# First stage of a graph network kernel: GpSimd takes over small table work from VectorE, the fall test moves, and fewer count columns

## The reference, cut to what matters

```python
h = jnp.maximum(_layernorm(x, axis=-1), 0.0)
x = x + _L0_gnn_ref(h, src, dst, ...)     # hn = layer_norm(h); ft = hn @ W_att; softmax over each
                                          # destination's edges of <ft[src], ft[dst]>; sum of ft[src]; MLP
h = jnp.maximum(_layernorm(x, axis=-1), 0.0)
x = x + _L1_gnn_ref(h, src, dst, ...)     # four convolutions over the same edges
```

## Time and profile before

| | us |
|---|---|
| median of 3 executions | 3775.62 |
| lowest and highest of them | 3770.89, 3781.33 |
| the profiled execution | 3790.5 |
| its span, first to last instruction | 3788.6 |
| of it, first stage with its barrier | 117.67 |

### The profile page before, as it was taken

One profiled execution on the slowest core, in us unless ns is written; L12 is line 12 of the kernel. 1 busy time (PEld: TensorE's weight loads), 2 busy tenths in 40 slices (PEclk: granted clock), 3 DMA queues, 4 the chain that ended last, 5 costly groups with the idle time before them and its releaser, 6 DMA issues. The chain is left out here.

```text
span 3788.6 us, 59184 instructions
## 1 busy us (share of the span) xinstructions
PE 3354.5 (89%) x20346; PEld 2097.6 (55%) x20346; DVE 2355.1 (62%) x3512; ACT 1776.8 (47%) x4853; POOL 2445.6 (65%) x2604
## 2 busy tenths in 40 slices
PE   5788888888888888888888787999999999999999
PEld 4566666666666666666655554444544454445444
DVE  8788888888888888888865574222422242224223
ACT  4788888888888878787744353000200020002000
POOL 2577777777777777777777001777277737764775
PEclk7688888888888888888887798999999999999999
DMA  7443334333333333334332415888688868877886
GB/s 207 125 108 103 107 104 107 104 107 104 107 104 107 104 107 104 107 104 124 103 85 60 62 51 169 254 254 256 215 255 254 253 215 254 256 248 229 259 264 192
DMA packets 491674, 599.98 MB, mean 158 GB/s; under 512 B 61546, under 2 KB 422613, under 8 KB 491103
## 3 DMA queue, kind: packets, MB, share of 16 engines
q1 hardware_dynamic: 355798, 337.71, 29.3%
q0 software_dynamic: 82960, 172.57, 18.4%
q10 hardware_dynamic: 52632, 86.13, 6.3%
HBM read 488.79 MB, written 109.00 MB: 158 GB/s over the span
## 5 line engine op out<-in xcount | busy, mean ns | idle before, releaser
L1001 POOL DMA_INDIRECT fts<-ft_tab,src_all x1568 | 1481.2, 945 | 477.7 <-issue 477.1
L2702 PE MATMUL cv_acc<-cv_cnt,cv_parts 128*128 128x512 bf16 x3960 | 864.0, 379 | 0.0
L2453 POOL DMA_INDIRECT cv_slots<-hs_tab,slot_idx x640 | 604.8, 945 | 195.1 <-issue 195.1
L1033 DVE TENSOR_TENSOR ohk<-iota_ps,key_cols 128x784 bf16<-128x784 f32 x704 | 651.1, 966 | 5.5
L2702 PEld LDWEIGHTS cv_acc<-cv_cnt,cv_parts 128*128 128x128 bf16 x3960 | 387.2, 98 | 464.6
L1457 PE MATMUL agg_ps<-terms,oh 128*64 128x141 f32 x2744 | 557.1, 378 | 75.6 <-DVE terms L1070 75.3
L1457 PEld LDWEIGHTS agg_ps<-terms,oh 128*64 128x64 f32 x2744 | 483.2, 189 | 116.3 <-DVE terms L1070 105.4
L1218 ACT ACTIVATE dist_l<-lo_iota,low 128x128 bf16<-128x128 f16 x1760 | 533.1, 387 | 16.5 <-ACT low L1213 0.4
L1397 PE MATMUL adj_ps<-ohk,ohl 128*128 128x196 bf16 x2816 | 378.2, 261 | 89.5 <-ACT strip L1270 46.8
L1270 ACT CAST strip<-adj_ps 128x392 bf16<-128x392 f32 x704 | 334.0, 474 | 239.5 <-PE adj_ps L1400 200.4
L2702 PE MATMUL cv_acc<-raw,cv_parts 128*128 128x512 bf16 x1920 | 420.9, 379 | 0.0
(11 more groups left out here) (350 smaller groups left out, 3592.1 us busy)
## 6 DMA issues: line engine op xcount, KB each, us to landing
cv_cnt<-adj SPq DMA_DIRECT2D x44, 2176.0 KB
cv_cnt<-adj SPq DMA_DIRECT2D x44, 2048.0 KB
raw<-adj SPq DMA_DIRECT2D x44, 2048.0 KB
adj<-strip ACTq DMA_DIRECT2D x176, 392.0 KB
fts<-ft_tab,src_all POOLq DMA_INDIRECT x1568
win<-ft_tab SPq DMA_DIRECT2D x196, 65.0 KB
hs_tab<-cv_hs ACTq DMA_DIRECT2D x24, 448.0 KB, 3.5
cv_slots<-hs_tab,slot_idx POOLq DMA_INDIRECT x640
```

Of the source, the lines that this page charges most:

```text
L1001: nc.gpsimd.indirect_dma_start(fts[u][:, k, :], None, ft_tab[:, :], bass.IndirectOffsetOnAxis(src_all[:, n, k:k + 1], 0)).then_inc(gathere ...
L1033: nc.vector.tensor_tensor(ohk[:, k.s, at, :], key_no.unsqueeze(1).to_broadcast([P, QC, KEYS]), columns(key_cols, k)[:, at].unsqueeze(2).to ...
L2453: nc.gpsimd.indirect_dma_start(slots[n % RING][:, e, :], None, hs_tab[:, :], bass.IndirectOffsetOnAxis(rows_at, 0)).then_inc(slots_in[n % ...
L2702: last = nc.tensor.matmul(a[:, 0:width], parts[:, r, b, :], cnt[q][:, 0:width // SUB, (b - b0) * SUB:(b - b0 + 1) * SUB], start=(b == 0 an ...
```

## The change

GpSimd makes what VectorE made in `spot_columns`, `rows`, `schedule` and most of `oddities`. It does the first ahead of its two conversions, and the others right after them and ahead of the fetches. Where VectorE had one fused instruction of two operations with a scalar per partition, GpSimd has separate ones: `rows` subtracts the centre with a tensor_tensor over all 2048 columns first. On VectorE `find_falls` moves from cycle 5 to after the loop, followed by one reduction over the odd marks (`count_odd`), both ahead of the last `turned_features`; the rest of `oddities` (`finish`) stays behind it. Counts, bounds and odd marks run over NHD = 1408 strips in place of NH = 1568.

```diff
-CQ = ((0, 393), (393, 392), (785, 392), (1177, 392))
+CQ = ((0, 353), (353, 352), (705, 352), (1057, 352))
...
-        thr = sb("thr", [P, NH + 1], FP16, c)
+        thr = sb("thr", [P, NHD + 1], FP16, c)
...
+            def spot_columns():
+                link(nc.gpsimd.tensor_scalar(side[:, 1:2], place[:], float(WD), None, ALU.is_ge))
...
+                last.then_inc(s["spots_made"], 1)
+
+            def rows():
+                pool.wait_ge(s["dst_f"], 1)
+                link(nc.gpsimd.tensor_scalar(centre[:], dst_f[:, :, 0], float(MID), None, ALU.add))
+                link(nc.gpsimd.tensor_tensor(dst_f[:], dst_f[:], centre[:].unsqueeze(2).to_broadcast([GH, 2, GE]), ALU.subtract))
+                for half in range(2):
+                    for a in range(2):
+                        last = nc.gpsimd.tensor_scalar(
+                            group_rows[:, half, 2 * a, :].rearrange("g (c p) -> g c p", p=P),
+                            dst_f[:, half, :].rearrange("g (p c) -> g c p", p=P)[:, a * (GC // 2):(a + 1) * (GC // 2), :],
+                            float(MID), None, ALU.min)
+                link(last)
+                for a in range(2):
+                    last = nc.gpsimd.tensor_tensor(group_rows[:, :, 2 * a + 1, :], group_rows[:, :, 2 * a, :],
+                                                   group_rows[:, :, 2 * a, :], ALU.mult)
+                last.then_inc(s["rows_made"], 1)
+
+            def schedule():
+                pool.wait_ge(s["ends_in"], 7 * 16)
+                nc.gpsimd.memset(delta_f[:], 0.0)
...
+            def oddities():
+                spans, strips = odd[:, 0:NG], odd[:, NG:NG + NHD]
+                pool.wait_ge(s["starts_made"], 1)
+                nc.gpsimd.tensor_tensor(strips, start_f[:, 1:NHD + 1], start_f[:, 0:NHD], ALU.subtract)
...
+                link(nc.gpsimd.tensor_tensor(spans, last_f[:], base_f[:], ALU.subtract))
+                nc.gpsimd.tensor_scalar(spans, spans, float(WD - 1), None, ALU.is_gt)
+                nc.gpsimd.tensor_scalar(strips, strips, float(SW - COARSE) / COARSE, None, ALU.is_gt
+                                        ).then_inc(s["odd_made"], 1)
+            spot_columns()
             pool.wait_ge(s["by_src_in"], 96)
             nc.gpsimd.tensor_copy(src_f[:], by_src[:]).then_inc(s["src_f"], 1)
             pool.wait_ge(s["by_dst_in"], 96)
             nc.gpsimd.tensor_copy(dst_f[:], by_dst[:]).then_inc(s["dst_f"], 1)
+            rows()
+            schedule()
+            oddities()
...
             def find_falls():
+                dve.wait_ge(s["ends_in"], 7 * 16)
...
-            def oddities():
...
+            def count_odd():
+                dve.wait_ge(s["odd_made"], 1)
                 link(nc.vector.tensor_reduce(irr_part[:], odd[:], AX.X, ALU.add))
+
+            def finish():
                 dve.wait_ge(s["base_summed"], 1)
...
-                if i == 1:
-                    dve.wait_ge(s["pool_const"], 2)
-                    spot_columns()
                 if i == 3:
-                    schedule()
-                if i == 4:
-                    rows()
-                if i == 5:
-                    find_falls()
+                    turned_spots()
+            find_falls()
+            count_odd()
             turned_features(NB - 1)
-            oddities()
+            finish()
```

More of the change, by code:

```diff
@@ L342, in _ @@
             nc.gpsimd.tensor_copy(ident_bf[:], ident[:]).then_inc(s["pool_const"], 1)
+            def spot_columns():
+                link(nc.gpsimd.tensor_scalar(side[:, 1:2], place[:], float(WD), None, ALU.is_ge))
+                link(nc.gpsimd.tensor_scalar(side[:, 0:1], side[:, 1:2], -float(WD), None, ALU.mult))
+                link(nc.gpsimd.tensor_tensor(place[:], place[:], side[:, 0:1], ALU.add))
+                link(nc.gpsimd.tensor_scalar(place[:], place[:], -float(MID), None, ALU.add))
+                link(nc.gpsimd.tensor_scalar(side[:, 0:1], side[:, 1:2], -1.0, 1.0, ALU.mult, ALU.add))
+                link(nc.gpsimd.tensor_tensor(spot_cols[:, 4:5], place[:], place[:], ALU.mult))
+                nc.gpsimd.tensor_scalar(spot_cols[:, 4:5], spot_cols[:, 4:5], -1.0, 1.0, ALU.mult, ALU.add)
+                for a in range(2):
+                    link(nc.gpsimd.tensor_tensor(spot_cols[:, 2 * a:2 * a + 1], side[:, a:a + 1], place[:], ALU.mult))
+                    nc.gpsimd.tensor_scalar(spot_cols[:, 2 * a:2 * a + 1], spot_cols[:, 2 * a:2 * a + 1], 2.0, None, ALU.mult)
+                    last = nc.gpsimd.tensor_scalar(spot_cols[:, 2 * a + 1:2 * a + 2], side[:, a:a + 1], -1.0, None, ALU.mult)
+                last.then_inc(s["spots_made"], 1)
@@ L511, in turned_sources @@
                                           ).then_inc(s["turned_out"], 1)
[L513 to L524, removed]
@@ L526, in schedule, with turned_spots, find_falls @@
-            def schedule():
+            def turned_spots():
                 dve.wait_ge(s["spots_turned"], 1)
                 nc.vector.tensor_copy(spots[:], base_ps[0:5, 0:P])
+            def find_falls():
                 dve.wait_ge(s["ends_in"], 7 * 16)
[L530 to L539, removed]
@@ L541, in rows @@
-            def rows():
-                dve.wait_ge(s["dst_f"], 1)
-                link(nc.vector.tensor_scalar(centre[:], dst_f[:, :, 0], float(MID), None, ALU.add))
-                for half in range(2):
-                    for a in range(2):
-                        last = nc.vector.tensor_scalar(
-                            group_rows[:, half, 2 * a, :].rearrange("g (c p) -> g c p", p=P),
-                            dst_f[:, half, :].rearrange("g (p c) -> g c p", p=P)[:, a * (GC // 2):(a + 1) * (GC // 2), :],
-                            centre[:, half:half + 1], float(MID), ALU.subtract, ALU.min)
-                link(last)
-                for a in range(2):
-                    last = nc.vector.tensor_tensor(group_rows[:, :, 2 * a + 1, :], group_rows[:, :, 2 * a, :],
-                                                   group_rows[:, :, 2 * a, :], ALU.mult)
-                last.then_inc(s["rows_made"], 1)
```

30 lines of the change are left out of this document (17 added, 13 removed).

## The result

| | before | after |
|---|---|---|
| median, us (7 executions each, taken in turn) | 3777.27 | 3787.55 |
| ratio after to before, 95% interval | | 1.0036 (1.002 to 1.0052) |
| profiled execution's span | 3788.6 | 3797.8 |
| first stage, start of the span to the first instruction of the next stage | 117.67 | 127.92 |
| attention, from there to some 2080 us | 1961.33 | 1961.08 |

A forecast was written before the change was run, and what follows sets the result against it. The first stage was taken to be bound by a full VectorE, which GpSimd's new work would hold: counts +9.8, oddities +4.4, pipeline −2.5, end 0, sum +11.7 us on the median 3775.6, so 3787.3 us; range 3774 to 3797.

The forecast's parts named there:

- Stage for stage, 1 us for 1 us: An earlier or later end of the first stage moves the whole rest of the kernel by the same amount.
- The stage's end: Last gap of VectorE: 5.4 us of work fits into 5.52, term 0; up to 1.5 us lost if TensorE is fast.
- The pipeline: From some 58 us ScalarE's three waits for VectorE go, a gain of 2.5 us.
- The reason given for moving the fall test: Left in cycle 5 of the pipeline, find_falls' 3.6 us would have been the next thing waited for.
- Fewer columns: One tenth fewer columns saves 1.9 us over 28 count steps, plus 0.2 for `thr` and starts.
- The counts: GpSimd's `rows` and `schedule`, 11.5 us, hold VectorE's count steps; 1.7 absorbed, so counts end 9.8 us later.
- The factor 1.85 for two operands: GpSimd's two-operand price, taken from VectorE's ratio of 1.771 to 0.957 us: 1.75 us per 1000 columns.
- TensorE follows: At the counts' end TensorE may finish 2 us behind VectorE, covered by the statistics, so no added cost.
- rival D: Dearer two-operand price, and TensorE, starved in the counts, falls to lower speed: +15 to +22 us, chance 0.21.
- Oddities: GpSimd's `oddities`, 4.6 us, holds VectorE's coefficients and edge keys: +4.4 us after 0.2 for shorter starts and `thr`.
- its last way to be wrong: GpSimd's instructions wait in VectorE's place, which would cost only the fetches' slack.
- C: The forecast case itself, GpSimd's work holding VectorE: +9 to +15 us, 3785 to 3791 us, chance 0.38.

The follow-up runs named there:

- e3: The changed kernel with only `rows` moved behind GpSimd's last fetch; ratio to the kernel before 1.0009, first stage from first count step 103.28 us (changed kernel 114.18).
- e8: The changed kernel with the four minima of `rows` reading 512 neighbouring columns in place of every eighth; first stage from first count step 113.77 us (changed kernel 114.18).
- e6: As e5, but with the fall test back in cycle 5 of the pipeline; first stage from first count step 103.24 us, 0.3 above e5.
- e2: The kernel before with only the counts, bounds and odd marks cut to 1408 strips; ratio to before 1.0003, first stage from first count step 101.17 us (before 103.57).
- e4: The changed kernel with strip bounds in PSUM as float32, each count step three plain-rate VectorE instructions; these took 693 ns beside `rows`, 692 with GpSimd idle.
- e1: The changed kernel with `rows`, `schedule` and `oddities` behind GpSimd's last fetch; ratio to the kernel before 1.0002, first stage from first count step 107.24 us.
- e9: As e5, with the fall test too behind the last turned features; ratio to the kernel before 1.0004, first stage from first count step 99.76 us.
- e10: The changed kernel with the fall test and reduction behind the last turned features, GpSimd's part untouched; first stage from first count step 113.14 us (changed kernel 114.18).
- e5: As e1, with the reduction over odd marks behind the last turned features; ratio to the kernel before 1.0003, first stage from first count step 102.97 us.
- e7: The kernel before with four GpSimd memsets of 98 x 2048 float32 added beside the counts; first statistics 29.38 us after the first count step, 9.0 later than before.

## Why the prediction was right, point by point

**Stage for stage, 1 us for 1 us:** held, 1961.33 and 1961.08 us for the attention.

**The stage's end:** held. SP waits 3.7 us for its last store again. The gap was filled to the edge: VectorE's features started at 118.50 us, TensorE's transposes had ended at 117.13 + 1.27 = 118.40. Of this trace the term of 0 is right; the loss named for a fast TensorE came in e3 (2.0 us) and in e8 (2.4 us, and a slower projection behind it), larger than the 1.5 us given.

**The pipeline:** −2.98 for −2.5 us. None of ScalarE's three waits is left after 72 us. A wait costs a little more than its idle time: the four rounds of ScalarE from 64.56 us took 8.09, 7.76, 8.27 and 9.81 us before, and each 7.75 or 7.76 us after, which is 2.9 us. The reason given for moving the fall test has e6 for it in kind, ScalarE's wait of 2.13 us; its size is open.

**Fewer columns:** 1.5 us at the counts (e2) for 1.9. The prediction read TensorE's pace as 0.60 us a step; that is VectorE's average with what it caught up. TensorE's own was 0.67 (its steps began at 19.54, 20.21, 20.88 us), so VectorE ended ahead of it. How much of this term is left in the changed kernel, where TensorE no longer paces the counts, no run shows.

**The counts:** +10.05 for +9.8 us, though two terms were wrong and in part made up for each other. From the starts of the count steps, at 0.50 us each:

| | predicted | measured |
|---|---|---|
| subtraction | 3.6 | 28.54 − 24.70 − 0.5 = 3.3 |
| four minima | 2.2 | 37.40 − 28.54 − 8 x 0.5 = 4.9 |
| two squares | 3.6 | 41.66 − 37.40 − 2 x 0.5 = 3.3 |
| `schedule` | 2.0 | 44.15 − 41.66 − 4 x 0.5 = 0.5 |
| absorbed | −1.7 | −1.9, what is left to +10.05 |

The mis-sized term is the minima. I priced a one-operand instruction by the conversions of the earlier trace rows (0.95 us per 1000 columns), with some 10% for the stride. Alone it takes 7.85 / 4 = 1.96 us for 512 columns (e4), four times the conversion's price. It held VectorE for less than its length: two count steps ran beside each. `schedule` takes GpSimd 4.0 us here, 2.5 alone (e1), but costs VectorE nearly nothing: there GpSimd gave way. The factor 1.85 for two operands was right: 3.60 us for 2048 columns, 1.76 us per 1000. The Trainium skill (GPSIMD Engine Reference, "Elementwise — side-by-side cycle accounting") gives 4497 ns for that; the measurement decides, 3.60 us. What the prediction made of that figure is too high besides: with the minima left at 2.2 us, `rows` comes to 11.4 us, not 12, and the sum to +14 to +15, not +15 to +16.

**TensorE follows:** wrong by 0.8 us. Its last matmuls came later than the statistics could cover, 0.92 us of waiting at 47.12. This is rival D's mechanism in half its size, as PE's timeline shows:

```profile
36.67 0.63 PE L711 MATMUL nf_ft_ps<-raw,ones_bf 128*128 128x353 bf16 x3 [0.56 <-DVE raw L536]
39.67 1.06 PE L711 MATMUL nf_ft_ps<-raw,ones_bf 128*128 128x353 bf16 x3 [1.35 <-DVE raw L536]
44.12 1.09 PE L711 MATMUL nf_ft_ps<-raw,ones_bf 128*128 128x353 bf16 x3
```

The granted clock was 1.00 from 34 to 39 us and 0.50 from 39.6 to 46 us, where the last steps of the counts stand.

**Oddities:** +2.59 for +4.4 us. The coefficients were held for 2.3 us, as said. The edge keys hardly were: the first three took 0.96 to 0.98 us each, as in the earlier trace rows, the conversion 1.25 for 0.98 and the last 1.93 for 1.78, 0.42 us in all. GpSimd's side stretched instead. Its timeline:

```profile
51.60 2.80 POOL L392 TENSOR_SCALAR odd<-base_f 1x1 f32<-1x1 f32 x2
54.46 2.15 POOL L394 TENSOR_TENSOR odd<-last_f,base_f 1x196 f32<-1x196 f32 x1
56.70 1.32 POOL L395 TENSOR_SCALAR odd<-odd 1x196 f32<-1x196 f32 x1
58.00 4.93 POOL L396 TENSOR_SCALAR odd<-odd 1x1408 f32<-1x1408 f32 x1
```

Two instructions of one element took 2.80 us, where e9 has 0.49, the subtraction over 196 columns 2.15, where e1 has 0.59, and the comparison over 1408 columns 4.93, where both have 3.76. `oddities` took GpSimd 13.9 us from 49.01, alone 8.3 (e9), and was priced at 4.6. So this term is wrong twice, in the price and in who waits, and +4.4 for +2.59 is near only because most of the real price fell on GpSimd. The prediction named this as its last way to be wrong, that GpSimd waits in VectorE's place; beside the edge keys it came true and cost only the fetches' slack: GpSimd was done at 62.93 and waited 3.60 us more for the keys. The Trainium skill (SBUF — State Buffer, "Who interferes with whom") says that whoever issues first has the ports for a whole instruction, and that a VectorE instruction with two SBUF inputs contends with GpSimd's reads. The trace agrees with both, the second with the held coefficients. It doesn't agree that the loser always blocks for the whole instruction: beside the minima VectorE got in midway.

**The cases:** C came, at the measured median 3787.55 us for 3787.3. Its error was 1.1 us on the sum of the stage, by luck in part: oddities came 1.8 us under their term and the pipeline 0.5, TensorE and the counts 1.1 us over theirs. That the median was hit to 0.3 us is luck too, as the kernel before now had a median 1.7 us higher than the one counted from.

## What to carry to other kernels

- Before work is moved to an idle engine, look in the trace for the moments when the two engines already work side by side: two stretched instructions out of two were enough to tell the direction of this result. An empty GpSimd is not free time if VectorE has fast SBUF instructions then and is the one that is late.
- Price a moved instruction by its own kind. A conversion, a two-operand and a scalar operation of one length stand at 1 to 2 to 3 here, the last at 4 with a stride. And the price falls on whichever engine waits, which has to be read for each neighbour by itself.
- A gap on an engine is as long as the other engine's wait makes it. Work put there to the edge is a risk of a few us wherever TensorE's speed varies; what ends after the last awaited transfer may stand there for nothing (e10).
- Before a gain of a few us in one trace is put down to a change, compare how long an untouched piece of work took in both: between e5 and e9 TensorE's last projections made the whole difference.

## What the runs showed of the hardware

- GpSimd holds back VectorE's fast SBUF instructions for the length of its conversions, subtractions, squares, and memsets that only write (2.25 us for 0.6, e7). It also holds VectorE instructions with two SBUF inputs at the plain rate: coefficients of 7 columns (2.48 us for 0.17), the fall test's first instruction (3.63 for 1.78, e9). It doesn't touch VectorE instructions that read PSUM at the plain rate (693 against 692 ns, e4), nor statistics that read one float32 input from SBUF (1.44 us, e5).
- Who waits is not fixed: beside `schedule` and the edge keys it was GpSimd (2.80 us for two instructions of one element, 0.49 alone).
- Each strided minimum of 512 columns (2.2 us) had two count steps beside it. Which property of the instruction lets VectorE in was not tried.
- Own prices on GpSimd: conversion and memset 0.9 to 1.0 us per 1000 columns, tensor_tensor 1.76 (float32) and 1.83 (float16), tensor_scalar 2.67 packed on one partition (3.76 us for 1408), 3.83 with a stride of 32 bytes on 98 partitions.
- TensorE's matmuls fell to the slower of two levels after it had waited for VectorE in the counts (granted clock 1.00, then 0.50), and were at either level in the same projection from kernel to kernel (1.80 or 3.1 to 3.4 us), which moved the last store by up to 3.9 us (e5, e9). What decides the level at the stage's end, these traces don't tell.
